# A GCN and mixture-of-experts kernel: the row that two windows share goes through DRAM into a spare operand row, and the dense chunks are cut anew

## What is computed

```python
def _gcn_layer(x, W, b, src, dst, norm, n_nodes):
    xt = x @ W
    msg = xt[src] * norm[:, None]
    agg = jax.ops.segment_sum(msg, dst, num_segments=n_nodes)
    return jax.nn.relu(agg + b)
...
norm = edge_weight * jax.lax.rsqrt(deg_out[src] * deg_in[dst] + EPS)
h6 = _gcn_layer(h5_all, W6, b6, src, dst, norm, N_NODES)
h7 = _gcn_layer(h6, W7, b7, src, dst, norm, N_NODES)
out = h7 @ Wp + bp
...
for e in range(E):
    h = jax.nn.gelu(jnp.einsum('bsd,dh->bsh', xn, W1[e]) + b1[e], approximate=False)
    y_e = jnp.einsum('bsh,hd->bsd', h, W2[e]) + b2[e]
    y = y + y_e * w_full[..., e, None]
```

## Time and profile before

| | us |
|---|---|
| median of 3 executions | 3186.37 |
| lowest and highest | 3182.78 and 3190.39 |
| span of the profiled execution, first to last instruction | 3189.0 |
| PE busy | 2693.2 (84%) |
| PE weight loads busy | 2024.6 (63%) |
| POOL busy | 1993.1 (63%) |
| DVE busy | 1895.4 (59%) |
| ACT busy | 856.2 (27%) |

### The profile page before, as it was taken

The page is one execution under the profiler, slowest core; times in us unless marked ns, Lnnn a source line. Parts: engine busy times, 40 slices in busy tenths (PEclk is TensorE's granted clock), DMA queues, the critical chain, the costliest instruction groups (busy, mean ns, idle before and its releaser), DMA issues. The chain is left out here.

```text
span 3189.0 us, 53553 instructions
## 1 busy us (share of the span) xinstructions
PE 2693.2 (84%) x17249; PEld 2024.6 (63%) x17249; DVE 1895.4 (59%) x5984; ACT 856.2 (27%) x2004; POOL 1993.1 (63%) x1964
## 2 busy tenths in 40 slices
PE   4567489999999999986589999999988865899995
PEld 3456257667666666664367666666665652789984
DVE  8999878788787887864202545555444446532210
ACT  5677611111111111112200011101010000456652
POOL 0000277777777777777477777777777663467763
PEclk8799799999999999998899999999988985899998
DMA  4001355555655555558666667777756654344444
GB/s 128 0 24 41 116 184 190 177 191 194 197 195 195 195 195 188 191 172 270 200 231 219 219 220 226 225 226 227 256 184 222 214 180 127 67 71 71 72 68 115
DMA packets 196687, 532.68 MB, mean 167 GB/s; under 512 B 39708, under 2 KB 127412, under 8 KB 189652
## 3 DMA queue, kind: packets, MB, share of 16 engines
q0 software_dynamic: 103872, 256.67, 31.0%
q1 hardware_dynamic: 89828, 254.39, 21.9%
q10 hardware_dynamic: 2736, 18.48, 1.5%
HBM read 379.28 MB, written 156.50 MB: 168 GB/s over the span
## 5 line engine op out<-in xcount | busy, mean ns | idle before, releaser
L913 POOL DMA_INDIRECT arena<-table,src_i x1744 | 1701.6, 976 | 598.1 <-issue 525.8
L2007 PE MATMUL bank<-arena 128*128 128x257 f32 x4900 | 1242.4, 389 | 4.4 <-ACT zcd L1704 4.4
L2007 PEld LDWEIGHTS bank<-arena 128*128 128x128 f32 x4900 | 887.9, 192 | 218.7 <-issue 106.8
L1248 DVE TENSOR_TENSOR arena<-arena,bank 128x294 f32 x768 | 348.6, 454 | 230.0 <-PE bank L1994 152.8
L1994 PE MATMUL bank<-arena 128*128 128x294 bf16 x2304 | 419.0, 295 | 71.5 <-DVE arena L1248 37.7
L1994 PEld LDWEIGHTS bank<-arena 128*128 128x128 bf16 x2304 | 222.3, 99 | 229.7 <-DVE arena L1248 65.7
L1229 DVE SCALAR_TENSOR_TENSOR arena<-iota_f,arena 128x256 f32<-128x256 f32 x768 | 360.0, 469 | 0.0
L2027 PE MATMUL bank<-arena,s_all 128*32 128x257 f32 x3488 | 300.3, 414 | 39.1 <-DMA arena<-table,src_i 37.5
L1695 ACT COPY arena<-zero 128x2144 f32<-128x2144 f32 (+1 forms) x104 | 159.1, 1561 | 380.4 <-DMA chunks<-arena 232.9
L939 POOL DMA_INDIRECT acc<-arena x105 | 181.0, 1724 | 118.6 <-ACT arena L1812 89.7
L1966 PE MATMUL bank<-arena 128*128 128x150 bf16 x1616 | 149.5, 253 | 110.7 <-DVE arena L1078 80.9
(11 more groups left out here) (244 smaller groups left out, 2775.9 us busy)
## 6 DMA issues: line engine op xcount, KB each, us to landing
chunks<-arena SPq DMA_DIRECT2D x25, 3283.0 KB
arena<-chunks SPq DMA_DIRECT2D x24, 3283.0 KB, 13.5
arena<-table,src_i POOLq DMA_INDIRECT x1744
zsum<-zc SPq DMA_DIRECT2D x109, 128.5 KB, 3.3
zrow<-zsum SPq DMA_DIRECT2D x50, 257.0 KB, 4.4
arena<-in_W ACTq DMA_DIRECT2D x16, 512.0 KB, 17.5
rows_x<-arena SPq DMA_DIRECT2D x25, 264.0 KB
arena<-chunks ACTq DMA_DIRECT2D x2, 3283.0 KB, 12.7
```

The source lines that it names most:

```text
L913: pool.indirect_dma_start(gat[:, r, j, 0:D], None, table[L], bass.IndirectOffsetOnAxis(ap=src_i[:, col:col + 1], axis=0)).then_inc(gathere ...
L1248: dve.tensor_tensor(win, win, ps_b[t % len(ps_b)].rearrange("p (h w) -> p h w", w=TW), ALU.add).then_inc(added, 1)
L2007: last = pe.matmul(ps_ap, adj[:, c % 2, h, 0:P], xp[:, h], start=(h == 0), stop=(h == XB_ALL - 1))
```

## The change

1. The products with `csel` and `cseld` and their two tables are gone. The last row of the operand of the next product takes the shared row instead. For a pair of groups that is row 127 of `zs`: ACT copies only rows 0 to 126 of the sum, SP brings the row from `zsum` by a DMA of one row of 257 words (`carry_row`, at the place of the even group), and `combine` waits for it (`carried`). The placing matrix sends row 127 to row 0 of the result. For a chunk it is row 127 of the last block of `xp`, which holds no node (6250 nodes end before it): SP brings the row there (`carry_chunk`), the matrix has a 1 at that place, which ACT writes when it zeroes the last slice (two small copies more for a chunk), and the last of the 49 products waits for it (`chunk_carried`).
2. SP waits, ahead of each such DMA, until the last store of rows has landed (`z_stored`, `zd_stored`).
3. Layer 0 has 16 chunks of 31 tiles and 8 of 30 (736 tiles for 720), the late chunks have 18 and 30 tiles (48 as before). So layer 0 has 110 groups and layer 1 has 104; the loop keeps its 96 groups, the tail has 14 turns, of which 8 take pairs of blocks.
4. Layer 1's first eight chunks go over three slots, the other 18 over four: 96 slots with a chunk for 98.
5. The limits of the check are by one row tighter, and a few operations of the set-up go and come.

```diff
-CHUNKS = 24
-CT = 30
-DT = CHUNKS * CT
-LATE_CHUNKS, LATE_CT, SHORT = 2, 24, 6
+LONG_CHUNKS, LONG_CT = 16, 31
+CHUNKS, CT = 24, 30
+DT = LONG_CHUNKS * LONG_CT + (CHUNKS - LONG_CHUNKS) * CT
+LATE_CT, SHORT = (18, 30), 8
...
+            def carry_row(L, n):
+
+                sp.wait_ge(z_stored[L], n // 2 * 16 + 16 * ZERO_FILLS[L])
+                row = zsum[L][bass.ds(group_base(L, n), 1), :] if n else zsum[L][ZROWS - 1:, :]
+                sp.dma_start(zs[P - 1:P, :], row).then_inc(carried, 16)
+
             def store_group(L, n):
                 if n % 2 == 0:
-                    return
...
+                    return carry_row(L, n)
...
+            def carry_chunk(L, c):
+
+                sp.wait_ge(zd_stored[L], 16 * c)
+                if 0 < c < N_CHUNKS[L] - 1:
+                    row = zsum[L][bass.ds(chunk_base(c), 1), :]
+                else:
+                    row = zsum[L][ZROWS - 1:, :]
+                sp.dma_start(xp[P - 1:P, XB_ALL - 1, :], row).then_inc(chunk_carried, 16)
...
                         if step == 0 and c >= 0:
                             store_chunk(c)
+                            carry_chunk(0, c)
...
                 sp.wait_ge(p_stored, 16 * NPAIR)
+                carry_chunk(1, 0)
                 store_chunk(ALL - 1)
...
                         if c + 1 < ALL:
                             load_chunk(c + 1)
+                        carry_chunk(1, c)
...
-                act.copy(zs[:, :], ps_seg).then_inc(zs_ready, 1)
+                act.copy(zs[0:P - 1, :], ps_seg[0:P - 1]).then_inc(zs_ready, 1)
...
                 for h in range(first_of_step(step), first_of_step(step + 1)):
+                    if h == XB_ALL - 1:
+                        pe.wait_ge(chunk_carried, 16 * (L * CHUNKS + c + 1))
                     last = pe.matmul(ps_ap, adj[:, c % 2, h, 0:P], xp[:, h], start=(h == 0), stop=(h == XB_ALL - 1))
-                    if h == 0 and c < N_CHUNKS[L] - 1:
-                        pe.matmul(ps_ap[0:1, :], cseld[:, c:c + 1], zcd[:, (c + 1) % 2], start=False, stop=False)
...
-                if n > 1 and second:
-
-                    pe.wait_ge(zc_ready, s)
-                    first = (G0[L] + n) // 2
-                    pe.matmul(ps_seg[0:1, :], csel[:, first:first + 1], zc[:, 1 - s % 2], start=False, stop=False)
...
+                    pe.wait_ge(carried, 16 * (s + 1))
                     pe.matmul(ps_z, cm[:, s % 2], zs[:, :], start=True, stop=True).then_inc(z_mm, 1)
```

More of the change, by code:

```diff
@@ L42 @@
 LOOP_GROUPS = 96
-GROUP_AT = [CT * h + 7 * s + 4 for h in range(2) for s in range(GPI // 2)]
+GROUP_AT = [(h, 7 * s + 4) for h in range(2) for s in range(GPI // 2)]
 FIRST_GROUPS_AT = [5 * s + 18 for s in range(GPI)]
@@ L152, in gnn_moe_kernel @@
         ccol = sb("ccol", [P, GALL // 2])
-        csel = sb("csel", [P, GALL // 2])
-        cseld = sb("cseld", [P, ALL])
+        not_last = sb("not_last", [P, 1])
         bg_i = sb("bg_i", [P, GALL // 2], I32)
@@ L552, in chunk_start @@
         def chunk_start(c):
-            return CT * min(c, CHUNKS) + LATE_CT * max(c - CHUNKS, 0)
+            return (LONG_CT * min(c, LONG_CHUNKS) + CT * max(min(c, CHUNKS) - LONG_CHUNKS, 0)
+                    + sum(LATE_CT[:max(c - CHUNKS, 0)]))
         def chunk_of(t):
-            return t // CT if t < DT else CHUNKS + (t - DT) // LATE_CT
+            return next(c for c in range(ALL) if t < chunk_start(c + 1))
         def group_no(L, n):
@@ L1694, in zero_chunk @@
             def zero_chunk(c, first, last):
-                act.copy(adj[:, c % 2, first:last], zero[:, :].unsqueeze(2).broadcast_to([P, last - first, AWID])
-                         ).then_inc(zeroed, 1)
+                whole = min(last, XB_ALL - 1) - first
+                done = act.copy(adj[:, c % 2, first:first + whole],
+                                zero[:, :].unsqueeze(2).broadcast_to([P, whole, AWID]))
+                if last == XB_ALL:
+                    act.copy(adj[:, c % 2, XB_ALL - 1, 1:], zero[:, :].broadcast_to([P, AWID - 1]))
+                    done = act.copy(adj[:, c % 2, XB_ALL - 1, 0:1], ident[:, P - 1:P])
+                done.then_inc(zeroed, 1)
             def copy_chunk(L, c):
```

130 lines of the change are left out of this document (69 added, 61 removed).

## The result

| | before | changed |
|---|---|---|
| median of 13 runs each | 3187.59 us (3182.78 to 3196.78) | 3208.87 us (3194.64 to 3221.49) |
| ratio to before | 1 | 1.0064 (95% interval 1.0051 to 1.0078) |
| span of the profiled execution | 3189.0 us | 3205.0 us |

The account below looks back on a forecast made before the run. It took PE and POOL's gathers as nearly equal bounds in layer 0's loop, and PE as layer 1's bound to 2300 us. Layer 1 (-31 + 18 + 9 = -4) and layer 0 (-3) gave 3179 us; range 3146 to 3220.

Parts of the forecast that it names:

- Layer 0's loop: Layer 0's loop ends when the gathers let it, their pace unchanged and DVE with room; the lag is gained: -5 us.
- the slower one (3215 us): Layer 1: the row lands with the matrix's last share or after it, 57 us of stalls before cover; 3215 us, chance 28%.
- Products that go: Removing csel and cseld products saves PE 39 us in layer 1 and 38 us in layer 0.
- so layer 1 is PE's: Layer 1 to 2300 us: PE, busy 656 of 723 us, sets the time, while POOL waits for nobody.
- Fewer groups: Layer 1 has two slots less, saving two sums, a placing product and their waits: 4 us.
- The row behind the matrix: Layer 1: the group's row, queued behind a matrix load, lands 12.6 us after that load's issue and stalls PE: +18 us.
- The first rival: Layer 1: the row passes the matrix or lands before it is wanted, so 18 and 9 us vanish; 3152 us, chance 25%.
- The new waits and the clock in layer 1: Layer 1: PE's waits ahead of each chunk's last product cost 9 us; three new clock falls cost 9 us (0 to 25).
- The tail's last store: End of layer 0's tail: the second of the last two stores now needs the first landed, then the row: +3.3 us.
- Layer 1 in all: Layer 1's sum: -31 for lighter PE work, +18 for the row, +9 for the clock, giving -4 us.

Follow-up runs that it names:

- the aligned loads: Changed kernel, with DVE loading tile offsets at tiles 0, 11 and 22 of each chunk instead of every tenth tile counted from the first: 3181.77 us, ratio 0.9971.
- the kernel with the later store: Changed kernel, with the store of a chunk's matrix in layer 0's loop waiting for four more tiles of the next chunk: 3196.76 us, ratio 1.0005.

## Why the prediction was wrong, point by point

**Layer 0's loop: the step that failed.** The working was that the gathers' pace does not change, so that the gain is the lag, -5 us, and that DVE has room with 807 of 1014 us busy. Both halves are sums over the stretch. The gathers' pace is a bound only as long as nothing else is late, and DVE's room was counted in busy time, in which register loads don't appear. The loads were in the trace of before (77 of them, up to 4.6 us in the loop), and laid beside the matrix stores they would have shown the drift. It cost 24 us (the aligned loads give them back; the loads moved into the store put 50 us on the kernel before). None of my rivals had it: the slower one (3215 us) named a time close to the result, for 57 us of waits in layer 1, where 33 came.

**Products that go: 39 us on PE, 31 us in the sum.** The price per product was near (PE's busy time is 33 us less without the products in layer 1, which I priced at 39, and 58 us less without any, priced at 77), but it was no time of the kernel: 4 us (0.9988), or 14 of 41 when put back. The step that failed is "so layer 1 is PE's". I had read that POOL waits for nobody and took PE to be the bound because it was the fuller one, 656 of 723 us. A POOL that waits for nobody and sets the pace of 10.1 us a group is the bound, as long as PE's distance behind it stays under the ring's four groups; in the kernel before it lay between 8 and 28 us from the 20th to the 80th group, and grew to 44 us only behind it. The earlier trace rows and the gathers' row hold this: 548 us busy and 1.26 us from one to the next. It is a reading of the kernel before up to its 88th group. In the changed kernel PE's waits for the row and the slots with a third of a chunk use the distance up, and POOL waits for PE 17.5 us in the first 80 groups.

**Fewer groups: 4 us in the sum, some 43 us in fact.** This is the term that I had furthest off in layer 1. The changed kernel gathers 832 tiles there and not 848, and 16 x 1.26 = 20 us of the gathers' own pace go (an estimate from the rows). I had priced the two slots by what PE does in them. The runs give more: from the old chunks to the new, with the row first in both, it is 1.35% (1.0043 to 0.9908). The other half is POOL's wait for PE behind the 80th group, 37.6 us against 8.1. The new chunks with the old products were not tried.

**The row behind the matrix: 18 us, and 20 to 22 measured.** This term held, in mechanism and size: 32.8 us of waits in 17, up to 3.6 us each, where the working had 36 us, all in slots behind a matrix load, of which 20 us arrive. The landing assumed at 12.6 us after the load's issue shows in the placing products, which started 11.9 to 14.0 us after it in the fifteen chunks of slots 24 to 80. The Trainium skill ("DMA: Bandwidth & Descriptors", "Why a DMA increments its semaphore by 16 and not by 1") says that a one-row DMA needs only one ring's share of what is ahead; by it the row comes with one of the shares of the matrix and not with the last. The trace agrees: of the seven four-slot matrices from 1926 to 2423 us whose landing it has, four landed 1.0 to 1.8 us behind the row, by the start of the placing product, three within 0.1 us of it, and none clearly ahead of it.

**The first rival's "vanish".** With the row issued first the waits did vanish and the time is 3164 us, not far from the rival's 3152; but what it holds is some 20 us of waits and some 43 us of the new cut, not the 34 us of products.

**The new waits and the clock in layer 1: 9 and 9 us.** PE never once waited for the chunk's row (no such row in its waits). The clock there went from 0.94 to 0.93 up to 2300 us and from 0.82 to 0.85 behind it, less than counted.

**The tail's last store: +3.3 us.** The term held. In the changed kernel PE's last wait for a row in layer 0 is the 4.9 us at 1578 us, and its last two placing products start 7.4 us apart, the 7 us of the sum. An earlier wait in the tail is 0.7 us; in the kernel with the old chunks it is 7.2, and that depends on where the groups fall.

**Layer 1 in all: -4 forecast, -8 measured**, and this was luck: the products' gain stood some 25 us or more too high, that of the groups and the new cut some 40 too low, and the two costs beside the row's wait, 18 us, have nothing that shows them but the carry's 10 us.

**All steps in one line**, each from one run's ratio to the next, so only good to some 0.2%: no products +0.1%, the rows through DRAM instead +0.3, the new chunks -1.35, the row behind the matrix +0.6, the loads that drift +0.9; together the +0.64% of the change.

## What to carry to other kernels

A period that divides another (ten offsets a load, thirty tiles a chunk) is part of the schedule, even if no line says so: when a size changes, list everything that recurs with it, put each next to the large transfers, and look where it drifts to. Ask of every saving which engine waits for nobody in that stretch: in most of layer 1 that is POOL, and 39 us off PE were worth 4 us, while two groups less with the new cut of the chunks were worth 43. A small transfer that someone is waiting for goes ahead of a large one on the same queue, and a stall in one piece costs where the same time in two pieces, each within the slack of the next engine, costs nothing.

## What the runs showed of the hardware

A load of ten registers from on-chip memory, 1.1 or 2.3 us by itself, took up to 9.7 us when it began 0.8 us behind the issue of a 3283 KB store from the same memory, and one of five registers 3.6 to 4.6 us. With ten registers 1.7 us ahead of the store's issue it took 2.8 to 3.6 us in most chunks, 0.4 to 0.8 us ahead of it 1.1 to 5.2 in the last chunks of the kernel with the later store, and 8 us or more behind it 1.1 to 5.0 in nearly all. In the profile such a load is a stop of DVE "for issue" and no busy time. With constant tile distance only every second store had this effect in full (8.7 to 9.7 us, then 1.4 to 3.8), and why is open. PE's granted clock fell to half (1.2 of 2.4 GHz) around the end of the long stop that is shown above: PE stood from 1290.2 to 1297.4 us, and from 1294 to 1301 us the mean granted clock is 0.52, ahead of it and behind it 1.00 and 0.99.
